# A diffusion-transformer kernel: feed forward by token groups with the next norm inside, the last group's norm moved into the causal attention, and everything from one norm to the recurrence's tables in one stage

## The reference, cut to what matters

```
x = x + y_cross + ff_b2 + (a * gelu(g)) @ ff_w2        # a, g: halves of h @ ff_w1 + ff_b1
e = norm(x); f = norm(e) * gain + bias                 # "norm twice"
y = causal_attention(f)                                # q, k normalised and scaled, masked softmax
g = norm(y) * gain + bias
p = softmax(g @ gate_w + gate_b)                       # 8 experts, dense
y = sum_e p[e] * (gelu_tanh(g @ w1[e] + b1[e]) @ w2[e] + b2[e])
x = x + norm(y) * gain + bias
i = norm(x)                                            # input of the recurrence, token by token
tables: score_w = W^T ctx,  gate_w = ctx @ kernel + bias
for t in 512: state = gru(state, i[t], attention(state, score_w, gate_w))
```

## Time and profile before

| what | us |
|---|---|
| median of 3 runs | 2856.56 |
| the profiled execution: its own time | 2861.57 |
| its span, first to last instruction | 2859.7 |
| feed forward, `norm_twice`, causal attention | 687 to 733.2, to 745.7, to 843.6 |
| "ln_g" and gating, experts | to 857, to 919.4 |
| "ln_h" and "ln_i", tables | to 930.3, to 936.4 |
| recurrence: set-up; steps | to about 943; to 2745 |
| last norm and second set of experts | to 2859.7 |

### The profile page before, as it was taken

How to read it: one execution, slowest core, us unless ns; L and a number is a source line. 1 busy time by engine, 2 the same in 40 slices (tenths; PEclk the granted TensorE clock), 3 DMA queues, 4 the chain that set the end, 5 groups by cost and what they waited for, 6 DMA issues and landing times. The chain is left out here.

```text
span 2859.7 us, 137627 instructions
## 1 busy us (share of the span) xinstructions
PE 2469.7 (86%) x57364; PEld 1677.2 (59%) x57364; DVE 1893.9 (66%) x7219; ACT 1576.0 (55%) x5266; POOL 992.2 (35%) x1992
## 2 busy tenths in 40 slices
PE   6999999988778899798999898898879877666669
PEld 4666666676445455565555565666656555444449
DVE  4666666785452677677677677677767765776553
ACT  4777777643443566576666575666657543333322
POOL 2000000042010467466677465566636411010126
PEclk9999999999989899999999999999999999999989
DMA  4000000000011100011000011000001000000013
GB/s 152 5 5 5 8 5 5 2 12 1 14 39 38 56 14 18 11 36 38 26 14 17 8 43 32 23 14 14 8 6 36 13 20 7 6 7 7 6 49 87
DMA packets 51897, 64.78 MB, mean 23 GB/s; under 512 B 7432, under 2 KB 36560, under 8 KB 51152
## 3 DMA queue, kind: packets, MB, share of 16 engines
q1 hardware_dynamic: 47184, 50.32, 5.9%
q0 software_dynamic: 4096, 5.67, 1.0%
HBM read 46.38 MB, written 9.60 MB: 20 GB/s over the span
## 5 line engine op out<-in xcount | busy, mean ns | idle before, releaser
L2167 POOL TENSOR_TENSOR gru_terms<-gru_states,gru_signs 128x8 f32<-128x8 f32 x512 | 104.1, 203 | 796.1 <-DVE gru_states L2452 691.3
L1908 PE MATMUL gru_ps_sr<-score_w,gru_states 128*32 128x78 f32 x4096 | 175.7, 243 | 182.4 <-DVE gru_states L2452 172.8
L2087 ACT ACTIVATE gru_p_t<-gru_ps_tc,gru_negmax 128x12 f32<-128x12 f32 x512 | 138.8, 271 | 342.5 <-DVE gru_negmax L2421 327.3
L2090 ACT ACTIVATE gru_th_r<-gru_pre_r 128x32 f32<-128x32 f32 x512 | 119.2, 233 | 304.2 <-DVE gru_pre_r L2434 303.9
L2143 POOL TENSOR_SCALAR bg_probs<-bg_probs,bg_arsum 128x256 f32<-128x256 f32 (+2 forms) x192 | 240.9, 1255 | 86.2 <-DVE gru_c_in L2441 80.4
L1658 PE MATMUL gru_ps_tc<-ctx_gate_w,gru_p_t 128*4 128x64 f32 x12288 | 268.2, 220 | 1.4 <-issue 1.4
L1658 PE MATMUL gru_ps_sr<-ctx_gate_w,gru_p_t 128*4 128x34 f32 x12288 | 189.5, 195 | 77.0 <-ACT gru_p_t L2087 74.5
L1908 PEld LDWEIGHTS gru_ps_sr<-score_w,gru_states 128*32 128x32 f32 x4096 | 81.3, 107 | 292.0 <-DVE gru_states L2452 273.0
L313 ACT ACTIVATE self_probs<-self_sc,self_negmax 128x512 f32<-128x512 f32 x256 | 176.7, 698 | 111.7 <-DVE self_negmax L351 111.7
L1658 PEld LDWEIGHTS gru_ps_sr<-ctx_gate_w,gru_p_t 128*4 128x4 f32 x12288 | 120.2, 86 | 195.5 <-ACT gru_p_t L2087 179.0
L351 DVE TENSOR_REDUCE self_negmax<-self_sc 128x1 f32<-128x512 f32 x256 | 159.0, 683 | 111.1 <-PE self_sc L236 111.1
(11 more groups left out here) (420 smaller groups left out, 6540.8 us busy)
## 6 DMA issues: line engine op xcount, KB each, us to landing
bg_w<-in_moe_w SPq DMA_DIRECT2D x48, 256.0 KB, 3.0
bg_wa<-in_wqkv SPq DMA_DIRECT2D x24, 192.0 KB, 2.4
moe_w<-in_moe_w SPq DMA_DIRECT2D x16, 256.0 KB, 3.5
best_w_sb<-in_ec_w SPq DMA_DIRECT2D x16, 256.0 KB, 3.4
x_products<-late SPq DMA_DIRECT2D x16, 240.0 KB
late<-x_products SPq DMA_DIRECT2D x240, 16.0 KB
cross_scratch<-ctab_raw SPq DMA_DIRECT2D x16, 154.0 KB
cross_outs<-cross_scratch POOLq DMA_DIRECT2D x4, 576.0 KB, 6.0
```

Source lines behind the costliest of these rows:

```text
L1908: last = pe.matmul(ps_s[32 * b:32 * b + 32, :], state(t)[:, b:b + 1].broadcast_to([P, 32]), score_w[:, b, 0:CTX + 1], start=True, stop=Tru ...
L2087: act.activation(p_t[:], ps_t, ACT.Exp, bias=negmax[:, 0:1]).then_inc(s_exp, 1)
L2090: act.activation(th_r[:, 1:64:2], pre_r[:], ACT.Tanh, scale=0.5).then_inc(s_thr, 1)
```

## The change

`feed_forward` goes by groups instead of batches, unrolled. `hidden` and `down` are doubled. While TensorE works on group g, the norm of group g-1 (both norms folded into one, as before) is done: sums and moments on VectorE between the second and the third gating product, the inverse root as a power on GpSimd, the scaling after the fourth, the transposes after the second layer of group g, the copy to `h_cols` on ScalarE one group later. Its SyncE queue loads the attention's first weights. The clearing of semaphores behind it is gone, and `norm_twice` too. The norm of group 3 goes into `first_causal`.

```
 feed_forward, TensorE:
+            for g in range(groups):
+                first_products(g)
+                second_product(g)
+                if g:
+                    turn_rows(g - 1)
 feed_forward, ScalarE:
+                    act.activation(gate[:, f % 2, :], gt[f % 2][:], ACT.Gelu, ...)
+                    if f == 1 and g > 1:
+                        take_cols(g - 2)
+            take_cols(groups - 2)
 feed_forward, VectorE:
+            for g in range(groups):
+                take_hidden(g, 0)
+                take_hidden(g, 1)
+                if g:
+                    add_down(g - 1)
+                    moments(g - 1)
+                take_hidden(g, 2)
+                take_hidden(g, 3)
+                if g:
+                    scale_rows(g - 1)
+                add_y(g)
+            add_down(groups - 1)
```

```
 first_causal, TensorE:
             project_v(0)
+            pe.wait_ge(s_nrows, 1)
+            for b in range(B):
+                last = pe.transpose(pt[:, place(b)], n_rows[:, b, :], ident)
+            last.then_inc(s_nturned, 1)
```

```
 first_tiles, TensorE:
+            table(0)
+            table(1)
+            turn_rows(0)
+            table(2)
+            ... lg: four logit products, two behind each half of the columns
+            first_product(0, range(2))
+            table(3)
+            pe.wait_ge(s_gates, 1)
+            ... four transposes of the gates
+            first_product(0, range(2, FC))
+            pe.wait_ge(s_gte, 1)
+            pe.wait_ge(s_tabled, 3)
+            ... four products with b2
             for e in range(E):
                 if e + 1 < E:
                     first_product(e + 1)
                 second_product(e)
+            pe.wait_ge(s_tabled, 4)
+            turn_rows(B)
 first_tiles, ScalarE:
+            act.preload_act_table_set("natural_log_exp_and_others")
+            deviations(L_G)
+            ... two copies of 256 columns into h_cols
+            act.wait_ge(s_gate, 3)
+            act.activation(expd[:], shifted[:], ACT.Exp).then_inc(s_gexp, 1)
             act.wait_ge(s_b1, 16)
             ... 32 gelus
+            act.preload_act_table_set("natural_log_exp_and_others")
+            deviations(L_H)
+            deviations(L_I)
 first_tiles, VectorE:
+            moments(L_G, y_tiles)
+            scale_rows(L_G, y_tiles)
+            for k in range(2):
+                take_table(k)
+            ... softmax of the gates; take_table(2); gates_t; take_table(3); y from the b2 products
             ... eight times four sums into y
+            moments(L_H, y_tiles)
+            ... four passes (y - mean) * gain, four passes * rstd + x
+            moments(L_I, x_tiles)
+            scale_rows(L_I, x_tiles)
```

In `recurrence` the set-up of VectorE is cut:

```
+            sp.wait_ge(s_spare, 2)
+            act.wait_ge(s_spare, 1)
+            pool.memset(x_rows, 0.0).then_inc(s_spare, 1)
+            pool.memset(spare[:, 0:2 * CHUNK * P], 0.0).then_inc(s_spare, 1)
-            dve.memset(ps_ox[:], 0.0).then_inc(s_init, 1)
-            dve.memset(spare[:, 0:2 * CHUNK * P + 4 * P], 0.0).then_inc(s_init, 1)
-            dve.memset(ps_tc[:, 0:P], -1e30)
-            dve.memset(ps_tc[:, P:BANK], 0.0).then_inc(s_init, 1)
-            dve.memset(ps_sr[:, 0:P + 32], 0.0)
-            dve.memset(ps_sr[:, P + 32:BANK], 1.0).then_inc(s_init, 1)
+            dve.memset(ps_own, 0.0).then_inc(s_init, 1)
+            dve.memset(ps_t, -1e30)
+            dve.memset(ps_cz, 0.0).then_inc(s_init, 1)
+            dve.memset(ps_sr[:, P:P + 32], 0.0)
+            dve.memset(ps_sr[:, P + 32:P + GATE_C], 1.0).then_inc(s_init, 1)
```

More of the change, by code:

```diff
@@ L451, in first_causal @@
         s_ot, s_oe, s_wd, s_y = (sem(n) for n in ("ot", "oe", "wd", "y"))
+        gain, bias = last_norm
+        n_stats, n_mv, n_var, n_rstd, n_power, n_rows = (sb(f"n_{n}", k) for n, k in (
+            ("stats", [P, B, 6]), ("mv", [P, B, 2]), ("var", [P, B]), ("rstd", [P, B]), ("power", [P, B]), ("rows", [P, B, P])))
+        s_nstats, s_naggr, s_npool, s_nrows, s_nturned, s_ncols = (
+            sem(f"n_{n}") for n in ("stats", "aggr", "pool", "rows", "turned", "cols"))
+        last_rows = x[:].rearrange("p (b t) d -> p b t d", t=NT)[:, :, NT - 1, :]
         block = ctx.enter_context(nc.Block())
@@ L880, in _, with feed_forward @@
             scale_rows(B - 1)
-def feed_forward(nc, spent, h_cols, x, y, weights):
+def feed_forward(nc, spent, h_cols, x, y, weights, ident, norm, ahead):
+    groups = NT
     with ExitStack() as ctx:
@@ L898, in feed_forward, with own, rows @@
         s_up, s_gelu, s_hid, s_down, s_y, s_y0 = (sem(n) for n in ("up", "gelu", "hid", "down", "y", "y0"))
+        s_power, s_stats, s_aggr, s_var, s_rstd, s_xn, s_turned, s_cols = (
+            sem(n) for n in ("power", "stats", "aggr", "var", "rstd", "xn", "turned", "cols"))
         block = ctx.enter_context(nc.Block())
+        tokens = h_cols[:].rearrange("p (b s) -> p b s", s=S)
+        def own(g):
+            return slice(g * P, (g + 1) * P)
+        def rows(of, g):
+            return of[:].rearrange("p (b t) d -> p b t d", t=NT)[:, :, g, :]
@@ new lines, in _ @@
+            take_cols(groups - 2)
+        @block.gpsimd
+        def _(pool):
+            pool.memset(power[:], -0.5).then_inc(s_power, 1)
+            pool.wait_ge(s_power, 1)
+            for g in range(groups - 1):
+                pool.wait_ge(s_aggr, g + 1)
+                pool.tensor_scalar(var[:], mv[:, :, 1], 1.0 + EPS, EPS ** 2, ALU.mult, ALU.add).then_inc(s_var, 1)
+                pool.wait_ge(s_var, g + 1)
+                wait_positive(pool, s_xn, g)
+                pool.tensor_tensor(rstd[:], var[:], power[:], ALU.pow).then_inc(s_rstd, 1)
@@ new lines, in scale_rows @@
+            def scale_rows(g):
+                dve.wait_ge(s_rstd, g + 1)
+                wait_positive(dve, s_turned, g)
+                for b in range(B):
+                    last = dve.tensor_scalar(xn[:, b, :], rows(x, g)[:, b, :], mv[:, b, 0:1], rstd[:, b:b + 1], ALU.subtract, ALU.mult)
+                last.then_inc(s_xn, 1)
+            dve.wait_ge(s_w, 48)
+            for g in range(groups):
+                take_hidden(g, 0)
[8 more added lines that the diff above has]
+                add_y(g)
@@ L952, in first_experts, with first_tiles, sb @@
+            add_down(groups - 1)
+def first_tiles(nc, spent, name, h_cols, x, y, x_t, gates, w1, w2, weights, norm, gating, tables, ident, ahead):
     w1_sb, w2_sb, b1_sb, s_w, s_b1 = weights
+    eps, gain, bias, g_rows, b_rows = norm
+    gw, gb_rows, b2 = gating
+    ctx_t, ctx_k, w_t, k_ctx, bias_rows, is_key, score_w, gate_w = tables
     RING = len(s_w)
     with ExitStack() as ctx:
+        def sb(n, shape):
+            return ctx.enter_context(nc.sbuf_tensor(f"{name}_{n}", shape, F32))
```

436 lines of the change are left out of this document (223 added, 213 removed).

## The result

The changed kernel takes 2823.22 us (median of 4 runs, 2822.87 to 2823.74), the kernel before 2857.52 in the runs beside it (2854.36 to 2858.54): a ratio of 0.9884, 95% interval 0.9871 to 0.9896. By the ratio that is 33 us, by the medians 34. Forecast were 2825.5 us and 31.1 us off.

A forecast was written before the change was run, and what follows sets the result against it. No engine bounds the whole; the recurrence is a chain of short operations across four engines. Terms 10.6 + 1.5 + 8.0 + 8.3 + 2.7 = 31.1 us off 2856.56 give 2825.5 us, range 2818 to 2836.

The forecast's parts named there:

- A: Feed forward and first norm: norm hidden beside TensorE's work, causal attention starts earlier, 10.6 us off.
- B: Start of the causal attention: first products run faster if TensorE's clock holds, 1.5 us off.
- the case in which the clock is kept: Causal attention's start: TensorE keeps full clock over a short gap, saving 2.3 us on products and square sums.
- C, first half: From the norm to expert 0's second layer: interleaved gating starts that layer earlier, 8.0 us off.
- Its other case: Same stretch with TensorE at half clock until 851: second layer of expert 0 at 860.9, gain 6.7 us.
- Rival 2: Interleaved gating: TensorE's in-order queue is held by the gates, gain there 4 instead of 8, time 2829.5; chance 0.12.
- C, second half: From the experts' last sum to the recurrence: shorter norms 2.6, clearing and barrier -0.2, tables beside gating 5.9; together 8.3 us.
- D: Recurrence's set-up: less clearing on VectorE, step 0's exponential at 4.3 us instead of 7.0, 2.7 us off.
- Rival 3: Recurrence's set-up: step 0 waits for loads rather than VectorE, so nothing is gained there, time 2828; chance 0.08.
- Rival 4: The 512 recurrence steps stretch; 0.061 us a step loses the gain, 0.1 gives 2876; chance 0.04.
- The windows' sum: Recurrence, step 0 to last step: the forecast is wrong if its windows differ by more than 3 us from 1801.

The follow-up runs named there:

- gates first, table loaded: Changed kernel with gates transposed ahead of all of expert 0's first layer and gelu's table loaded behind the gates' exponential: 2824.12 us.
- C alone: Kernel before with only the stretch from the norm through first experts and gating to the tables put in one stage: 2841.23 us, ratio 0.9950.
- D alone: Kernel before with only the recurrence's set-up taken from the changed kernel: 2854.41 us, ratio 0.9992.
- e0: Not a run but a measured interval: first load of the norm and experts to expert 0's second layer; 23.94 us before, 14.73 in the changed kernel.
- the kernel with the gates first: Changed kernel with TensorE waiting for the gates and transposing them ahead of all of expert 0's first layer: 2823.78 us.

## Why the prediction was right, point by point

- **A**, forecast 10.6, measured 10.46. The transposes cost 0.35 us a group (10.64 to 11.00) and not 0.51, 1.05 for 1.5. What the prediction did not have is the load of gelu's tables: the first group takes 13.83 us to the next one's first product where the first batch took 12.95, with no transposes in it, and the rows above show the load behind the first product and TensorE waiting 1.13 us. Some 0.9 us of A are lost there; an explicit load ahead of the stage, as in "gates first, table loaded", was not tried. That A came out near is so in part luck: 0.45 too much against 0.88 left out, and the rest in the hand-over.
- **B**, forecast 1.5, measured 1.98, the case in which the clock is kept. The transposes cost nothing that can be read.
- **C, first half**, forecast 8.0, measured 9.21. The term was mis-sized by hedging between two clocks; at full clock the prediction's own sum was 9.1. Its other case, 2.4 us later if half clock lasts until 851, did not come even where the stage began at 0.50: that cost 0.5 to 0.6 (15.24 and 15.30), as the clock was back at 1.00 some 4 us in. Second layer at 14.73 us, forecast 15. Rival 2 (TensorE held by the gates) did not come: the one wait left in this stretch is 0.27 us. The load of tables started 0.11 us behind the exponential's end, so the 1.4 us of drain per switch that the Trainium skill gives (ScalarE: Activation LUTs, "What ACT_TABLE_LOAD costs") is not seen here either.
- **C, second half**, forecast 8.3, measured 7.52. The two norms take 7.9 us (895.52 to 903.43), forecast 7.6. The boundary behind them is 1.65 (903.43 to 905.08) for 1.05, where I took 0.2 more: clearing the feed forward's semaphores is postponed, not removed. C alone has 8.1.
- **D**, forecast 2.7, measured 3.36. Here the size was near by luck and the step was wrong: "Next in line is ScalarE: `bg_b` lands at 2.7, load 1.28, its exponential 0.23". That load came from the tables that ScalarE was left with before, and C changes these. It would have been right for D alone (4.23 us, forecast 4.3). In the whole the next limit was VectorE behind GpSimd's 2048 columns: "SyncE's wait holds back nothing" and the clearing's 2.1 us were priced for the engines that wait on its semaphore, and the engine that shares its port was not thought of. It costs 0.7 us (3.67 to 2.95), and the load of 1.28 that did not come outweighs it.
- **Rival 3** is rejected (su 7.03 to 3.67). **Rival 4**, stretched steps, holds for the first eight alone, by 1.6 us in this execution. The prediction had nothing for these. The experts' loads had been in front of the first stores in the kernel before too, but the last had landed 3.4 us behind step 0's exponential, ahead of the first store at 3.6; now it lands at 7.0, with the store at 3.7. D alone has them side by side as well and lost nothing (30.42), so this is a likely cause and not a shown one.
- **The windows' sum** (1801 runs to the end of the last step): from step 0's exponential to that of step 511 it went from 1798.8 to 1795.9, 2.8 us less, just inside the 3 us set. The thirteen kernels with an edit lie between 1791.3 and 1798.3.
- **The sum.** The parts give 30.9, forecast 31.1. That this is so near is luck: the terms were off by -0.1, +0.5, +1.2, -0.8 and +0.7, and the first steps by -1.6. The further 2 to 3 us of the runs' medians lie in none of the priced parts; whether they are chance or come with C (8-511 above) is open.

## What to carry to other kernels

Read such a change as distances between the starts of stages, not as run times: here ff, sc, nt and su mostly repeat to 0.1 us between kernels that share them, where the runs scatter by several. Read the clock of a stage beside its length: ca and e0 do not repeat, by up to 2.5 us, with the clock. When several parts are priced from one profile of before, ask of each limit ("next in line is ...") whether another part of the same change removes it: the tables left by the last activation, the semaphores still to be cleared, perhaps the queue ahead of the first store. A clearing that is moved to an idle engine has to be put where the engine that shares its port has nothing urgent, and a load of tables that stands with its first user should be issued by hand as soon as the last user of the old set is done; the changed kernel still leaves one behind the feed forward's first product.

## What was not expected of the hardware

- GpSimd's memset of 2048 columns (1.83 us) held VectorE's 128-column scalings for 0.97 us instead of 0.17, and a copy of four elements for 1.85 instead of 0.17; VectorE's memsets ran beside it.
- A load of tables that nobody issues by hand waits for the operand of its activation: at 837.08 instead of some 834.9, 2.1 us later, in the kernel with the gates first, and at 690.09, 4.12 us idle behind the wait, in the feed forward of the changed kernel.
- Clearing semaphores is not free: the boundary of 1.05 us grew to 1.65 with those of the feed forward added. Without clearing a boundary took 0.3 us (734.05 to 734.32).
- The same stretch of the causal attention, TensorE busy for 4.3 of the 7 us before it, ran at a granted clock of 1.00 in one kernel's execution and 0.51 in another's; ca is 2.3 to 2.5 us longer for it.
- The recurrence behind step 8, instruction by instruction the same, differed by 7 us between the profiled executions of different kernels (1761.0 to 1768.3). That is more than part D.
